# Vision tower kernel: first tile's keys right behind its convolutions, its later steps among the second tile's products

## The chip, the core and the metric

One core of a Trainium2 chip runs the kernel. The metric is device time in microseconds (us), the median of 3 runs. PE is the matrix engine (TensorE), DVE the vector engine, ACT the scalar engine, POOL GpSimd, SP the queue that issues loads and stores.

## What is computed

`x` holds 64 images of 3 x 96 x 96, all weights are float32. A convolution with patches of 14 x 14 gives 6 x 6 = 36 rows of 256 channels for each image. They form 4 windows of 9 rows. Cut to what matters here:

```
red   = mean of the 9 rows of a window
q     = LN(red) @ la_wq ;  k, v = LN(rows) @ la_wkv
agg   = softmax(q . k / 16) over the 9 rows, 8 heads, times v
local = red + agg @ proj_w + proj_b
patch = local @ mod_w + mod_b                       (4 tokens)
cls   = class_emb + attention(class query, LN(local)) @ ga_proj   (1 token)
h     = [cls_tok, patch, cls]                       (6 tokens)
h     = h + causal attention(LN(h)) @ Wp + bp       (16 heads)
h     = h + top-2-of-8 experts(LN(h))
```

## The kernel before

**Rows and tiles.** The 64 images x 4 windows are 256 pairs; two tiles ("wt" 0 and 1) of 128 pairs each. Each tile has 9 convolution tiles of 128 rows, so there are 18, in 6 groups of 3 (`GT`): groups 0 to 2 are the first tile, 3 to 5 the second. Tokens 1 and 2 come from the first tile, 3 and 4 from the second, and 0 and 5 (class) from a third.

**Products in float32r pieces.** Convolutions, keys/values and the experts split each operand into a high and a low piece and sum three products (`PRODUCTS`). ACT writes the high piece (`patches_hi`, `turned`), DVE or POOL subtracts it for the low piece (`patches_lo`, `turned_lo`). `patches_lo(1)` and `(2)` are DVE's, 3 to 5 POOL's (`POOL_FROM`).

**Steps of a group.** PE `conv` (L429), ACT copies the rows out of the bank (`conv_copy`, L804), POOL sums the window (`window_sum`, L1068), DVE takes the moments (`group_moments`, L1197), POOL the reciprocal root (L1054). PE turns the rows (`turn_group`, L453) into banks 2 and 3, ACT and DVE make the two pieces (L845, L1317), PE multiplies by `wkv` (`keys_values`, L506, banks 4 to 7), ACT scales the result out (`keys_values_copy`, L865).

**Steps of a tile.** `window_mean` (DVE) normalises the mean row, `window_query_turn` and `window_query` (PE) give the query, `window_scores`, `score_maximum`, `window_weights` (DVE, L1237 to L1254, with one exponential on ACT) the weights. `value_product` (L355) multiplies values by weights, `value_sum` (L360) adds thirds, `tail_agg` (PE, L549) sums 128 x 128 blocks against the identity. For tile 0 the two sums leave 3 blocks (6 products); for tile 1, 6 blocks (12 products). Then come `tail_proj`, `local_out`, `tail_lo`, `tail_mod`, `pool_normalise`, `tail_pool`, `patch_out`, `in_normalise`, and for the tokens `turn_in`, `tile_qkv` (L628), `attention_products` (L376), `att_scores`, `att_weights`, `token_values` (L367), `turn_context` (L644), `out_proj` (L653), `residual`, `mid_normalise`, `turn_mid`, `router` (L667).

**What sets the order.** Each engine has one program, written out by hand, and runs it in order. Semaphores couple them; for the eight PSUM banks `FILLS` lists who writes a bank in which sequence, and `wait_free` makes the writer wait until all the writers ahead of it in that list have been copied out:

```
def wait_free(eng, b, name):
    n = FILLS[b].index(name)
    if n:
        eng.wait_ge(drained[b], n)
```

In bank 2 the list before runs turn0, turn1, turn2, redT0, turn3, and so on, and `turned_lo(g)` on DVE is what counts a turn as copied out. PE's list before runs: convolutions 0, 1, 2, keys 0, convolutions 3, keys 1, convolutions 4 (with the query of tile 0 between), keys 2, convolutions 5, keys 3, 4 and 5 (class products and the query of tile 1 between), then all that follows the weights of either tile. `keep_clock` (L674) issues products whose result nobody reads. From 130.9 us on runs the loop over 8 experts (L754, L767), with a prologue; the change does not touch it.

**Loads.** SP loads patches three groups ahead of their use, a group's buffer being free once the split of the group three before is done; the first experts' weights follow when all splits are done (issued at 50.3 us).

## Time and profile before

| what | value |
|---|---|
| median of 3 runs | 230.98 us (230.65 to 232.23) |
| the profiled execution's own time | 230.04 us |
| its span (first to last instruction) | 228.3 us |
| granted clock of PE, mean | 0.993 |
| busy PE / DVE / ACT / POOL | 202.4 / 157.0 / 101.3 / 95.7 us |

The span is what the trace covers; the execution's time is 1.74 us longer than it. A timeline row gives the start, the time from there to the end of the last of its merged instructions, the engine, the line, what is written and read, the shape, the count, and in brackets how long the engine stood idle before it and what ended that. Ends of PE rows are modelled, and overlap the next row's start a little: from start to start is the truer measure of a run of products.

### The profile page before, as it was taken

To read this page: it belongs to the slowest core of one execution; us is meant where nothing else is said; L and a number is where in the kernel's file an instruction comes from. 1 tells how busy PE (TensorE), PEld (TensorE's weight loads), DVE (VectorE), ACT (ScalarE), POOL (GpSimd) and SP (SyncE) were. 2 spreads that over 40 slices of the span, in tenths; PEclk is the share of its full clock that TensorE was granted. 3 is DMA by queue.
4 is the path that set the end of the run, shared out by engine and by line. 5 is a ranking of instruction groups with operands and counts; after the bars stand their busy time and mean duration, and the time that the engine had idled before them with its cause. 6 is when DMAs were issued, how large, how long until landed. Compare 5 with 4: busy or idle time off the path is not lost.

```text
span 228.3 us, 3936 instructions
## 1 busy us (share of the span) xinstructions
PE 202.4 (89%) x1332; PEld 186.4 (82%) x1332; DVE 157.0 (69%) x357; ACT 101.3 (44%) x225; POOL 95.7 (42%) x100
## 2 busy tenths in 40 slices
PE   1889979989999965878588889999999999999983
PEld 1888969877988845746376789999999999999983
DVE  2565880668388789477987599577856786867641
ACT  3665581825254633325221177283718371717120
POOL 0046099995236934355554314333333333333200
PEclk9999999999999998899999999999999999999999
DMA  6999920009400000000000004272534253400004
GB/s 219 342 384 372 317 95 3 3 17 364 173 0 1 3 0 0 0 0 0 1 3 0 0 3 157 120 279 38 239 97 179 41 235 82 194 0 0 3 0 69
DMA packets 4890, 23.01 MB, mean 101 GB/s; under 512 B 694, under 2 KB 2444, under 8 KB 3724
## 3 DMA queue, kind: packets, MB, share of 16 engines
q1 hardware_dynamic: 3960, 21.26, 26.8%
q10 hardware_dynamic: 916, 1.58, 2.0%
q8 instruction: 8, 0.13, 0.2%
q14 instruction: 6, 0.05, 0.1%
HBM read 22.44 MB, written 0.39 MB: 100 GB/s over the span
## 4 chain that ended last, share of the span: by engine, by line
PE 60%; DVE 13%; POOL 10%; issue 6%; ACT 4%; DMA 2%; SPq 2%; ACTq 0%; DVEq 0%; POOLq 0%
PE bank L754 25%; PE bank L767 15%; PE bank L506 5%; PE bank L429 4%; POOL split L1083 3%; POOL window L1068 3%; DMA raw<-xb 2%; PE bank L644 2%; DVE kv_rows L1237 2%; POOL rstd L1054 2%; PE bank L549 2%; PE bank L453 2%; DVE window L1211 2%; PE bank L653 1%; SPq L350 1%
## 5 line engine op out<-in xcount | busy, mean ns | idle before, releaser
L754 PE MATMUL bank<-split 128*128 128x322 f32 x384 | 59.2, 314 | 0.6 <-DVE vprod L1565 0.6
L754 PEld LDWEIGHTS bank<-split 128*128 128x128 f32 x384 | 57.6, 188 | 0.9 <-issue 0.9
L1182 POOL TENSOR_TENSOR split<-raw,split 128x256 fp32r<-128x256 f32 x32 | 29.0, 908 | 56.6 <-DVE split L1518 56.6
L767 PE MATMUL bank<-split 128*128 128x256 f32 x288 | 36.1, 283 | 0.6 <-DVE split L1571 0.6
L767 PEld LDWEIGHTS bank<-split 128*128 128x128 f32 x288 | 35.4, 192 | 0.8 <-DVE split L1571 0.8
L429 PE MATMUL bank<-split 128*128 128x256 f32 (+1 forms) x225 | 28.3, 284 | 1.8 <-POOL split L1086 1.2
L429 PEld LDWEIGHTS bank<-split 128*128 128x128 f32 (+1 forms) x225 | 27.5, 191 | 2.5 <-POOL split L1086 1.7
L506 PE MATMUL bank<-split 128*128 128x512 f32 x108 | 26.9, 399 | 0.0
L1021 ACT ACTIVATE vprod<-bank 128x322 f32<-128x322 f32 x32 | 13.9, 436 | 24.7 <-PE bank L754 24.6
L1565 DVE TENSOR_TENSOR vprod<-bank,vprod 128x322 f32<-128x322 f32 x32 | 15.7, 491 | 11.9 <-PE bank L754 8.3
L506 PEld LDWEIGHTS bank<-split 128*128 128x128 f32 x108 | 19.8, 188 | 3.9
L1513 DVE TENSOR_TENSOR split<-raw,split 128x512 fp32r<-128x512 f32 x29 | 20.7, 712 | 2.4 <-ACT split L891 2.3
L1029 ACT CAST split<-vprod 128x322 fp32r<-128x322 f32 x32 | 14.8, 463 | 16.3 <-DVE vprod L1565 16.2
L1054 POOL TENSOR_TENSOR rstd<-veps,mhalf 128x1 f32<-128x1 f32 (+2 forms) x17 | 11.3, 670 | 25.4 <-DVE veps L1204 25.2
L891 ACT CAST split<-raw 128x512 fp32r<-128x512 f32 x32 | 19.5, 614 | 2.6 <-DMA raw<-ffn_w 2.6
L1197 DVE BATCH_NORM_STATS2 stats<-pe_rows 128x6 f32<-128x256 f32 x24 | 9.0, 417 | 14.6 <-ACT pe_rows L804 14.4
L1557 DVE SCALAR_TENSOR_TENSOR pe_rows<-bank,wgt,pe_rows 128x256 f32<-128x256 f32 x24 | 11.2, 479 | 11.1 <-PE bank L767 11.1
L1571 DVE TENSOR_TENSOR split<-vprod,split 128x322 fp32r<-128x322 f32 x32 | 15.9, 497 | 1.4 <-ACT split L1029 1.4
L865 ACT ACTIVATE kv_rows<-bank,rstd 128x512 f32<-128x512 f32 x18 | 12.0, 691 | 8.4 <-PE bank L506 8.4
L1068 POOL TENSOR_TENSOR window<-window,pe_rows 128x256 f32<-128x256 f32 x14 | 11.7, 836 | 9.2 <-ACT pe_rows L804 8.1
L804 ACT COPY pe_rows<-bank 128x256 f32<-128x256 f32 x18 | 6.5, 374 | 19.0 <-PE bank L429 18.1
L444 PE MATMUL bank<-split 128*128 128x256 f32 (+1 forms) x45 | 8.2, 356 | 5.3 <-ACT split L818 5.3
(165 smaller groups left out, 287.4 us busy)
## 6 DMA issues: line engine op xcount, KB each, us to landing
raw<-ffn_w SPq DMA_DIRECT2D x8, 1536.0 KB, 6.5
raw<-xa SPq DMA_DIRECT2D x5, 768.0 KB
tok<-tok_w SPq DMA_DIRECT2D x1, 1536.0 KB, 12.9
tok<-tok_w SPq DMA_DIRECT2D x1, 776.0 KB, 6.7
raw<-xa ACTq DMA_DIRECT2D x1, 576.0 KB, 5.4
raw<-xb SPq DMA_DIRECT2D x6, 96.0 KB
att<-att_w SPq DMA_DIRECT2D x1, 488.0 KB, 14.4
raw<-conv_w SPq DMA_DIRECT2D x1, 384.0 KB, 5.9
```

Of the source, the lines that this page charges most:

```text
L429: mm = pe.matmul(bank[b][:, 0:C], xs[0:n, g % 2, px, a:a + P], cws[0:n, pw, k, :], start=(k == 0 and m == 0), stop=(k == len(KCH) - 1 and ...
L506: mm = pe.matmul(bank[b][:, :], lns[:, g % 2, px, a:a + P], wkvs[:, pw, aw:aw + 2 * C], start=(c == 0 and m == 0), stop=(c == CC - 1 and m ...
L754: mm = pe.matmul(bank[b][:, 0:NCOL], aws[:, q, pw, a:a + P], ms[:, px, c, FIRST:ROWS], start=(c == 0 and m == 0), stop=(c == CC - 1 and m ...
L767: mm = pe.matmul(bank[b][:, 0:C], hids[:, px, s * FQ + q, a:a + P], bws[:, s, pw, q * C:(q + 1) * C], start=(q == 0 and m == 0), stop=(q = ...
L891: act.copy(aws[:, q, HI, :], a_raw[:, slot, q, :]).then_inc(a_hi, 1)
L1029: act.copy(hids[:, HI, s * FQ + q, FIRST:ROWS], hidf[:, q % 2, :]).then_inc(hid_hi, 1)
L1054: pool.tensor_tensor(rstd[0:parts, k, 0:n], veps[0:parts, k, 0:n], mhalf[0:parts, 0:n], ALU.pow).then_inc(rstd_done, 1)
L1068: pool.tensor_tensor(redsum[:, wt, :], pe_rows[:, wt, 0, :] if n == 1 else redsum[:, wt, :], pe_rows[:, wt, n, :], ALU.add).then_inc(sum_s ...
L1182: pool.tensor_tensor(bws[:, s, LO, q * C:(q + 1) * C], b_raw[:, s, q, :], bws[:, s, HI, q * C:(q + 1) * C].bitcast(F32), ALU.subtract).the ...
L1513: dve.tensor_tensor(aws[:, q, LO, :], a_raw[:, slot, q, :], aws[:, q, HI, :].bitcast(F32), ALU.subtract).then_inc(a_split, 1)
L1565: dve.tensor_tensor(hidf[:, q % 2, :], bank[5 + q % 2][:, 0:NCOL], sg[:, q % 2, :], ALU.mult).then_inc(hid_done, 1)
L1571: dve.tensor_tensor(hids[:, LO, s * FQ + q, FIRST:ROWS], hidf[:, q % 2, :], hids[:, HI, s * FQ + q, FIRST:ROWS].bitcast(F32), ALU.subtract ...
```

## The change

PE runs keys 0, 1 and 2 and the query of tile 0 before convolutions 3; ACT and DVE follow. `patches_lo` 3 to 5 go from POOL to DVE, and tile 0's value products and sums too. The steps of tile 0 behind its weights (aggregate, projection, modulation, tokens 0 to 2, their attention, output projection and middle normalisation) are issued between convolutions 4 and the end of keys 5. Tile 1 gets no sums: `tail_agg(1)` takes 9 blocks (18 products) behind three value products on DVE. `token_values` of tokens 0 to 2 go from POOL to DVE. Banks and buffers are dealt out anew (`h0`, `pv0`; `lo` and `poolnorm` hold one tile), and functions that are only moved are not shown.

```diff
--- before.py
+++ after.py
-VSTEPS = 4
+VSTEPS = 5
 REST = KCH[-1][1]
 REST_PARTS = ((0, 64), (64, REST))
-POOL_FROM = 3
 AHEAD_A, AHEAD_B = 3, 2
...
-QKV = {"qkv_cls": (4, (0,)), "qkv0": (7, (1, 2)), "qkv1": (3, (3, 4)), "qkv_pool": (4, (5,))}
+QKV = {"qkv_cls": (2, (0,)), "qkv0": (3, (1, 2)), "qkv1": (3, (3, 4)), "qkv_pool": (4, (5,))}
...
-LNS = ["conv0", "conv1", "conv2", "conv3", "red0", "conv4", "class", "conv5", "red1",
-       "pool0", "pool1", "in0", "in1", "in2", "mid0", "mid1", "mid2"]
+LNS = ["conv0", "conv1", "conv2", "red0", "class", "conv3", "conv4", "pool0", "conv5", "red1", "in0", "mid0",
+       "pool1", "in1", "in2", "mid1", "mid2"]
...
-MOD_BANK = (6, 1)
-LO_BANK = (3, 0)
+AGG_BANK = (6, 2)
+PROJ_BANK = (7, 3)
+LO_BANK = (6, 6)
+MOD_BANK = (1, 7)
...
+    [f"conv{i}" for i in range(TILES) if CONV_BANK[i] == 2] + ["turn0", "turn1", "turn2", "redT0", "turn3", "turn4", "redT1", "turn5",
+                                                            "qkv_cls", "agg1", "poolT1", "wp1", "mid1"],
+    ["turn0", "turn1", "turn2", "q0", "turn3", "turn4", "q1", "turn5", "qkv0", "mid0", "proj1", "qkv1"],
...
-        lo = sb("lo", [P, 2, C])
+        lo = sb("lo", [P, C])
         loT = sb("loT", [P, CC, P])
-        poolnorm = sb("poolnorm", [P, 2, C])
+        poolnorm = sb("poolnorm", [P, C])
+        h0 = sb("h0", [P, C])
+        pv0 = sb("pv0", [P, BLOCKS[0][1] * (BLOCKS[0][1] + 1) // 2, HS * DV])
         poolT = sb("poolT", [P, CC, 2 * P])
...
-            elif g < POOL_FROM:
+            else:
                 eng.wait_ge(x_split, g)
-            else:
-                eng.wait_ge(x_split_pool, g - POOL_FROM + 1)
...
-                    elif wt == 1 and i == 0:
-                        pe.wait_ge(third_done, 2)
-                    elif wt == 1 and i == GT:
-                        pe.wait_ge(vprod_step, VSTEPS + 3)
+                    elif wt == 1 and i % GT == 0:
+                        pe.wait_ge(vprod_step, VSTEPS + 1 + i // GT)
...
             keys_values_group(0)
+            turn_group(2)
+            window_query_turn(0)
+            keys_values_group(1)
+            window_query(0)
+            keys_values_group(2)
             conv_group(3)
-            turn_group(2)
-            keys_values_group(1)
+            class_column()
             conv(GT * 4)
             conv(GT * 4 + 1)
-            window_query_turn(0)
-            conv(GT * 4 + 2)
-            window_query(0)
             turn_group(3)
-            keys_values_group(2)
-            conv_group(5)
-            turn_group(4)
-            class_column()
-            keys_values_group(3)
-            turn_group(5)
             pe.wait_ge(tok_rest_in, 16)
             class_query()
+            conv(GT * 4 + 2)
+            class_keys()
+            conv(GT * 5)
+            tail_agg(0, range(GT))
+            turn_group(4)
+            conv(GT * 5 + 1)
+            tail_proj(0)
+            conv(GT * 5 + 2)
+            tail_lo(0)
+            keys_values(GT * 3)
+            tail_pool(0)
+            tail_mod(0)
+            keys_values(GT * 3 + 1)
+            window_query_turn(1)
+            keys_values(GT * 3 + 2)
+            window_query(1)
+            turn_group(5)
             keys_values(GT * 4)
+            turn_in(0)
             keys_values(GT * 4 + 1)
-            window_query_turn(1)
-            keys_values(GT * 4 + 2)
-            window_query(1)
-            keys_values(GT * 5)
-            class_keys()
-            keys_values(GT * 5 + 1)
-            keys_values(GT * 5 + 2)
...
-            tail_agg(0, range(GT))
-            tail_proj(0)
             pe.wait_ge(att_in, 16)
             pe.wait_ge(tok_cols, 1)
             qkv("qkv_cls")
-            tail_agg(1, (*range(2 * GT, NW), *range(GT)))
-            tail_lo(0)
+            tile_qkv(0, "qkv0")
+            keys_values(GT * 4 + 2)
+            keys_values_group(5)
+            pe.wait_ge(dve_values, BLOCKS[0][1])
+            turn_context(0, 0)
+            out_proj(0, 1, [(0, "ctx0")])
+            turn_mid(0, 3)
+            tail_agg(1, range(NW))
             tail_proj(1)
...
-            pe.wait_ge(pool_values, BLOCKS[0][1])
-            turn_context(0, 5)
-            out_proj(0, 2, [(5, "ctx0")])
-            pe.wait_ge(pool_values, BLOCKS[0][1] + 1)
-            pe.wait_ge(dve_values, 1)
+            pe.wait_ge(pool_values, 1)
+            pe.wait_ge(dve_values, BLOCKS[0][1] + 1)
             turn_context(1, 6)
-            out_proj(1, 0, [(6, "ctx1")])
-            pe.wait_ge(dve_values, 2)
-            pe.wait_ge(pool_values, BLOCKS[0][1] + 2)
+            out_proj(1, 2, [(6, "ctx1")])
+            pe.wait_ge(dve_values, BLOCKS[0][1] + 2)
+            pe.wait_ge(pool_values, 2)
             turn_context(2, 5)
-            out_proj(2, 7, [(5, "ctx2")])
-            turn_mid(0, 3)
-            turn_mid(1, 2)
+            out_proj(2, 7, [(0, "ctx0"), (5, "ctx2")])
             pe.wait_ge(gate_split, 1)
             wait_free(pe, 4, "router")
             router(0, 3)
+            turn_mid(1, 2)
             keep_clock(6, 2)
             router(1, 2)
...
+            keys_values_copy(0)
+            turned(2)
+            two_pieces(2, "redT0", redT, "q_g", "q_b")
             patches_hi(4)
-            keys_values_copy(0)
-            conv_copies(3)
-            turned(2)
+            keys_values_copy(1)
+            query_copy(0)
+            keys_values_copy(2)
+            conv_copy(GT * 3)
+            window_exp(0)
+            conv_copy(GT * 3 + 1)
+            conv_copy(GT * 3 + 2)
             patches_hi(5)
-            keys_values_copy(1)
             conv_copy(GT * 4)
             conv_copy(GT * 4 + 1)
-            two_pieces(2, "redT0", redT, "q_g", "q_b")
+            turned(3)
             conv_copy(GT * 4 + 2)
-            query_copy(0)
-            turned(3)
-            keys_values_copy(2)
-            conv_copies(5)
+            conv_copy(GT * 5)
+            aggregate_copy(0)
             turned(4)
-            keys_values_copy(3)
-            window_exp(0)
+            conv_copy(GT * 5 + 1)
+            conv_copy(GT * 5 + 2)
+            copy_pair(LO_BANK[0], "lo0", loT)
+            keys_values_copy(3, 0)
+            patch_columns(0)
+            keys_values_copy(3, 1)
+            two_pieces(2, "redT1", redT, "q_g", "q_b")
+            keys_values_copy(3, 2)
+            query_copy(1)
             turned(5)
-            two_pieces(2, "redT1", redT, "q_g", "q_b")
-            keys_values_copy(4)
-            query_copy(1)
-            wait_full(act, CONV_BANK[TILES - 1], f"conv{TILES - 1}")
             weights_hi(0, 0, 16)
-            keys_values_copy(5)
...
+            keys_values_copy(4, 0)
+            hT_copy(0)
+            keys_values_copy(4, 1)
+            qkv_copy("qkv_cls")
+            qkv_copy("qkv0")
+            keys_values_copy(4, 2)
+            keys_values_copy(5, 0)
+            attention_exp(0)
+            keys_values_copy(5, 1)
+            keys_values_copy(5, 2)
+            context_copy(0, 0)
             window_exp(1)
+            experts_input_hi(0, 3)
             weights_hi(0, 1, None)
             weights_hi(0, 2, None)
             down_hi(0)
             down_hi(1)
...
-            attention_exp(0)
+            attention_exp(1)
             hT_copy(2)
-            attention_exp(1)
             qkv_copy("qkv_pool")
-            context_copy(0, 5)
+            context_copy(1, 6)
             attention_exp(2)
-            context_copy(1, 6)
             context_copy(2, 5)
-            experts_input_hi(0, 3)
             experts_input_hi(1, 2)
             experts_input_hi(2, 5)
...
-            patches_lo(3)
             window_sum(2)
             reciprocal_root("conv2", GT)
-            patches_lo(4)
+            reciprocal_root("red0", 1)
+            with_proj_bias(0)
+            reciprocal_root("class", 1, 2)
             window_sum(3)
             reciprocal_root("conv3", GT)
-            reciprocal_root("red0", 1)
-            patches_lo(5)
-            with_proj_bias(0)
             window_sum(4)
             reciprocal_root("conv4", GT)
-            reciprocal_root("class", 1, 2)
+            reciprocal_root("pool0", 1)
             window_sum(5)
             reciprocal_root("conv5", GT)
             reciprocal_root("red1", 1)
             with_proj_bias(1)
+            reciprocal_root("in0", 1)
...
+            out_bias(0, MOD_BANK[0], "mod0")
+            reciprocal_root("mid0", 1)
             weights_lo(0)
-            second_tile_third()
-            reciprocal_root("pool0", 1)
...
-            pool.wait_ge(att_step, ATT)
-            for t in (1, 2, 0):
-                values(t)
...
+            def value_products(wt):
+                dve.wait_ge(soft_step, SOFT * (wt + 1))
+                if wt:
+                    wait_full(dve, AGG_BANK[0], "agg0")
+                for k in range(GT):
+                    value_product(dve, wt, k).then_inc(vprod_step, 1)
+
+            def first_tile_sums():
+                for k in (1, 2):
+                    dve.wait_ge(vprod_step, 1 + k if k == 1 else VSTEPS - 1)
+                    value_sum(dve, k).then_inc(vprod_step, 1)
...
+            patches_lo(1)
+            group_moments(0)
+            patches_lo(2)
+            weights_centred()
+            turned_lo(0)
+            group_moments(1)
+            turned_lo(1)
+            group_moments(2)
+            window_mean(0)
+            patches_lo(3)
+            turned_lo(2)
+            dve.wait_ge(con_in, 32)
+            moments("class", [crow[0:2, :]], 2)
+            normalise("class", [crow[0:2, :]], [crow[0:2, :]], 2)
+            patches_lo(4)
+            window_scores(0, 0)
+            window_scores(0, 1)
+            window_scores(0, 2)
+            score_maximum(0)
+            window_weights(0)
+            value_products(0)
+            wait_full(dve, 5, "clsT")
...
+            dve.tensor_tensor(clsT[:, :], clsm[:, :], w_tok("gq_b"), ALU.add).then_inc(cls_step, 1)
+            patches_lo(5)
+            wait_full(dve, 5, "gq")
...
+            dve.tensor_tensor(gqblk[:, :, :], const("headmask").rearrange("p (c h) -> p c h", c=CC),
...
+            first_tile_sums()
+            group_moments(3)
+            wait_full(dve, 5, "u")
...
+            turned_lo(3)
+            group_moments(4)
+            turned_lo(4)
+            local_out(0)
+            group_moments(5)
+            pool_normalise(0)
+            window_mean(1)
             dve.wait_ge(bias_in, 64)
+            patch_out(0)
+            turned_lo(5)
+            in_normalise(0)
+            window_scores(1, 0)
+            dve.tensor_copy(hT[:, 0, :, :, :].rearrange("p c s b -> p c (s b)"), spread(tokT[:, :], 2, P)).then_inc(tok_cols, 1)
+            attention_products(dve, 0, ("qkv_cls", "qkv0")).then_inc(qk_dve, 1)
+            att_scores(0)
+            window_scores(1, 1)
+            att_weights(0)
+            att_wait(0, ATT)
+            for t in (1, 2, 0):
+                values(t)
+            window_scores(1, 2)
+            score_maximum(1)
+            residual(0, 1)
+            residual_moments(0, 1)
             window_weights(1)
+            value_products(1)
+            mid_normalise(0)
+            experts_input_lo(0, 3)
             local_out(1)
             pool_normalise(1)
             patch_out(1)
+            in_normalise(1)
...
-            residual(0, 2)
-            residual_moments(0, 2)
-            residual(1, 0)
-            residual_moments(1, 0)
-            mid_normalise(0)
+            residual(1, 2)
+            residual_moments(1, 2)
             mid_normalise(1)
             residual(2, 7)
```

## Rows read from the trace of the kernel before

**Rows 1.** Stretches (us): busy time (x instructions) of each engine, clock, DMA share, GB/s.

```profile
33.10:80.20 47.10, 44.73 (x279) 39.36 (x279) 29.50 (x64) 21.40 (x43) 33.31 (x33) 1.00 0.18 68
80.20:92.90 12.70, 8.07 (x46) 7.40 (x46) 11.15 (x19) 4.03 (x14) 5.53 (x4) 0.87 0.00 0
92.90:130.90 38.00, 29.82 (x161) 22.90 (x160) 28.37 (x70) 11.04 (x37) 17.57 (x21) 1.00 0.00 1
130.90:228.30 97.40, 92.63 (x672) 91.99 (x672) 67.18 (x161) 45.45 (x97) 27.55 (x30) 1.00 0.30 102
```

**Rows 2.** Timeline of PE: start, us, engine, line, shapes, xcount, idle before and what ended it.

```profile
28.14 0.82 PE L453 MATMUL bank<-con,pe_rows 128*128 128x128 f32 x6
...
28.71 4.34 PE L506 MATMUL bank<-split 128*128 128x512 f32 x18
...
34.30 5.65 PE L429 MATMUL bank<-split 128*128 128x256 f32 x45 [1.25 <-POOL split L1086]
...
49.29 0.44 PE L453 MATMUL bank<-con,window 128*128 128x128 f32 x2 [0.96 <-DVE window L1211]
...
80.24 1.58 PE L549 MATMUL bank<-con,vprod 128*128 128x128 f32 x12
...
88.29 4.54 PE L549 MATMUL bank<-con,vprod 128*128 128x128 f32 x24 [3.87 <-POOL vprod L355]
```

**Rows 3.** Stretches of PE: busy, granted clock, DMA share, GB/s.

```profile
84.40:88.30 3.90, 0.03 (x2) 1.00 0.00 0
88.30:92.30 4.00, 4.00 (x22) 0.61 0.00 0
```

**Rows 4.** Timeline of POOL and DVE, window sum, normalisation, splits.

```profile
34.21 2.49 POOL L1068 TENSOR_TENSOR window<-window,pe_rows 128x256 f32<-128x256 f32 x3
...
37.27 0.86 POOL L1054 TENSOR_TENSOR rstd<-veps,mhalf 128x3 f32<-128x3 f32 x1
...
12.59 1.76 DVE L1294 TENSOR_TENSOR split<-raw,split 128x1536 fp32r<-128x1536 f32 x1 [2.08 <-ACT split L827]
...
14.27 0.55 DVE L1296 TENSOR_TENSOR split<-raw,split 76x384 fp32r<-76x384 f32 x1
...
33.11 1.01 DVE L1317 TENSOR_TENSOR split<-bank,split 128x384 fp32r<-128x384 f32 x2
...
70.32 0.82 DVE L1211 TENSOR_SCALAR window<-window,mv,rstd 128x256 f32<-128x256 f32 x1 [0.67 <-POOL rstd L1054]
```

**Rows 5.** Timeline of PE, products that are moved.

```profile
94.52 1.03 PE L486 MATMUL bank<-tok,loT 128*128 128x256 f32 x4
...
101.00 1.75 PE L628 MATMUL bank<-att,tok 128*128 128x224 f32 x8 [0.51 <-ACT tok L950]
```

**Rows 6.** Timeline of DVE and POOL, scores, values, contention.

```profile
73.36 0.95 DVE L355 TENSOR_TENSOR vprod<-kv_rows,pn 128x768 f32<-128x768 f32 x1
...
75.84 2.53 DVE L1237 TENSOR_TENSOR kv_rows<-kv_rows,window 128x768 f32<-128x768 f32 x1 [1.53 <-ACT window L854]
...
78.41 0.95 DVE L1239 TENSOR_REDUCE sc<-kv_rows 128x24 f32<-128x768 f32 x1
...
108.04 0.74 DVE L1398 TENSOR_REDUCE kv_rows<-vprod 128x72 f32<-128x576 f32 x1
...
116.37 0.83 DVE L367 TENSOR_TENSOR window<-kv_rows 128x640 f32<-128x640 f32 x1
...
80.06 1.99 POOL L1144 TENSOR_TENSOR split<-raw,split 128x512 fp32r<-128x512 f32 x1
```

**Rows 7.** Timeline of DVE, POOL and PE, tail.

```profile
110.81 0.41 DVE L1483 TENSOR_TENSOR pe_rows<-bank,base 128x256 f32<-128x256 f32 x1
...
112.17 0.55 POOL L1054 TENSOR_TENSOR rstd<-veps,mhalf 128x1 f32<-128x1 f32 x1 [1.37 <-DVE veps L1204]
...
122.21 1.58 PE L644 MATMUL bank<-con,window 128*128 128x128 f32 x12 [0.17 <-issue]
...
130.06 0.83 PE L667 MATMUL bank<-gsplit,split 128*128 128x8 f32 x6
```

345 lines of the change are left out of this document (127 added, 218 removed).

## The prediction

> **What bounds the kernel now.** I read the stretches first [rows 1]: from 33.1 to 80.2 us PE is busy 44.7 of 47.1 us, so in the convolutions and keys every product that is added to PE's program lengthens it. From 80.2 to 92.9 it is busy 8.1 of 12.7 us and DVE 11.2: here the second tile's weights are the path. From 92.9 to 130.9 neither is full (29.8 and 28.4 of 38.0): a chain of short steps through all engines. The experts (97.4 us) are products back to back and untouched. Next the timeline of PE for the order and for what ended its waits [rows 2]: 1.25 us for POOL's split and 0.96 us for the normalised mean row in the full stretch, then 3.87 us until the second tile's values were weighted. Last the timelines of DVE, POOL and ACT for what is queued behind what. In short: the experts begin when four things in a row are done: the last keys product (80.2), the second tile's aggregate (92.85), and 38.05 us of tail.
>
> **Part 1, keys 0 to 2 right behind convolutions 2.** Turn 2 is issued at 33.05 and done at 33.6 (28.71 plus 4.34; a turn takes 0.57 from start to start [rows 2]). Next on PE stands the query's turn, redT0. It waits for the mean row: POOL starts the last sums at 29.7, is done 2.9 later, takes two reciprocal roots (0.86 and 0.56), and DVE normalises in 0.82 beside POOL's bias add [rows 4, 7]: 35.1. But redT0 is in bank 2 behind turn2, and turned_lo(2), which frees it, stands on DVE behind patches_lo(3): 1.76 + 0.5, then half of 1.01 [rows 4]. So redT0 goes at 37.7, and PE waits 4.1 us, with keys 1 queued behind, for which all was ready by 31. The old waits of 1.25 and 0.96 go, since convolutions 3 now come after two groups of keys. Net +1.9. Bounds: 0, if the idle stays as it was; +3.6, if the clock falls (rival below).
>
> **Part 2, the splits of groups 3 to 5 from POOL to DVE.** 2.3 us each on DVE in place of POOL's. DVE has room until 80.2 (29.5 busy of 47.1 [rows 1]); the only one that anyone waits for is that of part 1. POOL no longer holds DVE up in this stretch: 0, bounds -0.5 and +0.5.
>
> **Part 3, products moved before the last keys.** tail_agg(0) 12 records for about 1.35 [rows 2]; proj and mod, 4 records each, 0.9 each; qkv_cls and qkv0, 12 records at 1.75 for 8, make 2.4 [rows 5]; the turns lo, pool and in0, eight records or four blocks, 0.75 by redT0's spacing [rows 2]. Together 6.3 us on an engine that is full: all on the path. Bounds 5.6 and 6.5 (modelled ends).
>
> **Part 4, new waits of those products.** I walked the four programs against each other. tail_pool(0) waits for pool_normalise(0), which is queued on DVE behind group_moments(5), and that waits for the copy of the last convolution: 1.1 us idle, with tail_mod(0) and keys behind. turn5 in bank 3 waits for q1's copy 0.3; in0, behind turned_lo(5) on DVE, 0.1; qkv_cls waits for tok_cols behind window_scores(1, 0) 0.3. With less pieces of wait in between, +1.6; bounds 0 and 3. The other steps find their input ready: class products, agg0, proj0, lo0 (DVE reaches each 1 to 3 us ahead). Last keys product: 80.2 + 1.9 + 6.3 + 1.6 = 90.0.
>
> **Part 5, from the last keys to the second aggregate.** Before it took 12.65 us. Now DVE is the queue. It idles until qkv0 is copied out (85.1), then does the attention products (about 0.7) and scores of tokens 0 to 2 (0.74 and three steps of 0.25 [rows 6]), a third of the second tile's scores (0.95 twice [rows 6]), weights (0.9), their values (768 columns where 640 took 0.83 [rows 6], in three parts 1.3), the last third of scores 1.9, the maximum 0.6: it is at 93.9. There residual(0) waits for ctx0 (1.5), its copy (0.5) and out_proj(0) (1.1): 94.6; with its moments 1.3; window_weights(1) only then, 0.8: 96.7. Three value products at 0.95 [rows 6], where POOL has just started weights_lo(0), held back until now by mid0's root. Between rows here: DVE's two-input step took 2.53 beside POOL and 0.95 as a rule, the reduce 0.95 beside POOL also [rows 6]. I take 1.1 for it: 100.7. PE's turn_mid(0) waits for mid_normalise(0), behind all three, and tail_agg(1) behind it starts at 101.35, though the first third was ready at 98.8. It has 36 records in place of 24. PE will have idled nearly 7 us; after 3.9 idle the clock in the trace was 0.61 of full over the next 4 us [rows 3], and 24 records took 4.54 where 12 had taken 1.35 [rows 2]. So 4.05 at full clock and 1.7 for the clock: 5.75, to 107.1. That is 17.1 against 12.65: +4.45. Bounds: +1 (DVE's values overlap better, no contention, no fall) and +7.
>
> The Trainium skill bears on the step of 1.1: its page "SBUF — State Buffer", section "Who interferes with whom", says that a DVE instruction with two SBUF inputs and a GpSimd instruction that reads SBUF exclude each other for the whole instruction, whichever started first. By this rule the other order is as likely a price: had the value product started first, POOL would wait and the step cost nothing (239.2). The trace agrees with the rule as far as it goes (2.53 beside POOL, the reduce untouched).
>
> **Part 6, the tail.** What is gone: patch_out(0) with its moments and in_normalise(0), between pool_normalise(1) and the scores of the class query (about 1.3 by 110.81 to 112.17 [rows 7], and 0.7): -2.0 at gatt. The class row h2 was added at 110.81 [rows 7], held by att_scores(0) and POOL, though its product was ready at 109.2: -1.7. So the class row is normalised 16.7 after the aggregate in place of 20.3. ACT gives some back: attention_exp(1) stands before hT_copy(2), and context_copy(1) before attention_exp(2). turn_context(2) starts at +26.4 in place of +29.35 (122.21 [rows 7]). Then residual and norm of tile 0 are not in the way: the last router products end at +34.05 in place of +38.05 (130.06 + 0.83 [rows 7]). So -4.0, bounds -6 (hT_copy(2) costs nothing) and -2.5.
>
> **Sum**, against the profiled execution, 230.04 us (span 228.3 and 1.74 around it; 0.94 under the median, which I leave): +1.9 + 0 + 6.3 + 1.6 + 4.45 - 4.0 = +10.25, that is 240.3 us.
>
> **Rivals.**
> (a) The clock falls in the first wait too. For it: 3.9 us of idle did it at 84.4 [rows 3], and this one is 4.1 after full work. Against: before the old one PE was also thinly used. Price as there: half clock for about 3.4 us of records, +1.7: 242.0. The Trainium skill's "TensorE: Matmul & The Clock Gate", section "HAM oscillation — how this bites in real kernels", says the clock returns to its lower level after too long a gap and each gap pays anew; with its rule applied to both gaps the time is this one, 242.0.
> (b) The second tile's chain is no longer than it was. DVE finishes the first tile's attention beside the keys, as its 11 us of slack in the full stretch allow, and part 5 costs 0 to 1: 230.04 + 9.8 - 4.0 + 0.5 = 236.3. Against: the attention cannot start before qkv0 at 84.
> (c) Faster: the tail's relief outweighs. Place: the gaps of PE in 80.2 to 130.9, 12.7 us [rows 1]. If the moved products fill what was idle (part 3 costs 1 instead of 6.3, being issued where PE would have waited for DVE anyway), the old 3.87 us wait for POOL's product goes, and the first wait is hidden, the time is 230.04 + 1 - 3.9 - 4.0 = 223. It turns at the point where relief, 8, passes the costs before the aggregate; those I count at 14. Against it: 44.7 busy of 47.1.
> (d) Costs and relief cancel: query wait hidden, part 4 nothing, aggregate at full clock, tail -6: 230.04 + 6.3 + 1 - 6 = 231.3.
>
> **How the numbers follow.** The forecast 0.5, (a) 0.22, (b) 0.18, (c) 0.05, (d) 0.05. A measurement of this kernel tells about 1% from no change. (c) counts as faster; (d) as within 1%; 240.3, (a) and (b) as slower. Range: 236.0, just under (b), to 243.5, above (a) for part 4's upper bound.
>
> **What would show it.** In the changed profile: PE idle for about 4 us near 33.6 to 37.7, ended by DVE's turned_lo (L1317 of before); convolution groups unbroken; about 1 us idle before tail_pool(0); the last keys product at 90 (88 to 92); the second aggregate of 36 records starting near 101, ended by mid_normalise(0), at half clock first; the first expert product near 141. If PE has little idle before 80 and the last keys end near 86, parts 1 and 4 are wrong; if the aggregate starts within 8 us of the last keys, part 5 is; if the experts begin more than 36 or less than 32 us after it, part 6 is.

## The result, and the profile after

| | before | after |
|---|---|---|
| median | 230.81 us (4 runs) | 245.69 us (243.26 to 246.73, 4 runs) |
| ratio | 1 | 1.0643 [1.0585, 1.0702] |
| the profiled execution's own time | 230.04 us | 245.45 us |
| last keys product ends | 80.2 us | 92.4 us |
| second aggregate ends | 92.83 us | 110.14 us |
| first expert product | 130.75 us | 146.15 us |
| granted clock of PE, mean | 0.993 | 0.965 |

Medians are over all executions of a kernel; ratios and their 95% intervals leave out those more than 1.5% above its fastest one. The change makes the kernel slower by 6.4%. The direction was forecast, the size was not: 245.7 us stands above 240.3 and also above the range's end of 243.5.

The stretches of the kernel after, cut at the same four milestones as [rows 1] (columns as there). The experts' stretch is as before; everything is lost ahead of it.

```profile
33.10:92.40 59.30, 53.38 (x316) 46.30 (x314) 41.23 (x89) 27.69 (x60) 14.91 (x21) 0.94 0.14 54
92.40:110.20 17.80, 9.12 (x54) 8.29 (x54) 10.36 (x23) 3.57 (x10) 2.64 (x3) 0.81 0.00 0
110.20:146.20 36.00, 25.70 (x125) 19.27 (x125) 19.98 (x51) 7.28 (x25) 12.88 (x15) 0.95 0.00 0
146.20:243.70 97.50, 92.72 (x673) 92.08 (x673) 67.17 (x161) 45.55 (x97) 27.46 (x30) 1.00 0.29 102
```

The clock columns, 0.94, 0.81 and 0.95, where [rows 1] has 1.00, 0.87 and 1.00, are the first thing to see. The timeline of PE after, in the order in which the prediction walked it:

```profile
37.62 0.66 PE L456 MATMUL bank<-con,window 128*128 128x128 f32 x2 [4.02 <-DVE split L1296]
37.94 6.71 PE L509 MATMUL bank<-split 128*128 128x512 f32 x18
...
45.16 4.48 PE L509 MATMUL bank<-split 128*128 128x512 f32 x18
...
74.52 0.44 PE L456 MATMUL bank<-con,poolnorm 128*128 128x128 f32 x2 [1.40 <-DVE poolnorm L1183]
...
84.43 2.51 PE L592 MATMUL bank<-att,tok 128*128 128x224 f32 x12 [0.27 <-issue]
86.62 5.78 PE L509 MATMUL bank<-split 128*128 128x512 f32 x24
...
103.76 0.69 PE L456 MATMUL bank<-con,pe_rows 128*128 128x128 f32 x2 [6.12 <-DVE pe_rows L1183]
104.24 5.90 PE L550 MATMUL bank<-con,vprod 128*128 128x128 f32 x36
...
129.36 0.99 PE L592 MATMUL bank<-att,tok 128*128 128x224 f32 x4 [1.84 <-ACT tok L910]
131.66 3.90 PE L608 MATMUL bank<-con,window 128*128 128x128 f32 x18 [1.30 <-POOL window L370]
138.17 1.58 PE L608 MATMUL bank<-con,window 128*128 128x128 f32 x12 [1.01 <-DVE window L370]
```

The first wait is there as walked: 4.02 us, ended by DVE's low piece of turn 2. So is the long one before the second aggregate, 6.12 us, ended by the middle normalisation, with 36 records behind it. What the sum did not hold is in the durations: keys 1 took 6.71 us for 18 records where keys 2 behind them took 4.48, and the context turn of the second tile 3.90 for 18.

The stretches of PE after, around the three waits (busy, granted clock, DMA share, GB/s):

```profile
36.00:40.00 4.00, 2.38 (x7) 0.52 0.00 0
40.00:44.00 4.00, 4.00 (x12) 0.63 0.02 4
100.00:104.00 4.00, 0.24 (x1) 0.63 0.00 0
104.00:108.00 4.00, 4.00 (x21) 0.52 0.00 2
126.00:130.00 4.00, 1.39 (x7) 1.00 0.00 0
130.00:134.00 4.00, 2.69 (x13) 0.72 0.00 0
```

Three falls to the lower of the clock's two levels, 1.2 GHz, where [rows 3] shows one. The first two follow 4.02 and 6.12 us of idle. The third follows 4 us in which PE was busy 1.39, with gaps of 0.77, 1.84 and 1.30: no single long one. The 1.95 us that PE waited for the first context at 94.34 brought no fall (granted clock 1.00 from 94 to 98).

The timeline of DVE after, at the first wait and at the long one. In front of the low piece at 36.94 stand the split's 1.75 and 0.54, the queue of part 1. In front of the normalisation at 103.31 stand the three value products.

```profile
34.08 0.80 DVE L1183 TENSOR_SCALAR window<-window,mv,rstd 128x256 f32<-128x256 f32 x1 [0.67 <-POOL rstd L1067]
34.80 1.75 DVE L1273 TENSOR_TENSOR split<-raw,split 128x1536 fp32r<-128x1536 f32 x1
36.47 0.54 DVE L1275 TENSOR_TENSOR split<-raw,split 76x384 fp32r<-76x384 f32 x1
36.94 1.00 DVE L1296 TENSOR_TENSOR split<-bank,split 128x384 fp32r<-128x384 f32 x2
...
99.70 3.68 DVE L357 TENSOR_TENSOR vprod<-kv_rows,pn 128x768 f32<-128x768 f32 x3
103.31 0.40 DVE L1183 TENSOR_SCALAR pe_rows<-pe_rows,mv,rstd 128x256 f32<-128x256 f32 x1
```

### The profile page after: what moved, and what is told of

It reads as the page before. It is cut to its first block, busy times and chain, and to the rows that moved or that the text cites. A ratio compares the mean times of both kernels' runs of the same rounds, so it can differ in the third digit from the quotient of the medians.

```text
span 243.7 us, 3950 instructions
## 1 busy us (share of the span) xinstructions
PE 208.8 (86%) x1344; PEld 191.8 (79%) x1344; DVE 158.9 (65%) x370; ACT 102.0 (42%) x225; POOL 68.9 (28%) x86
## 4 chain that ended last, share of the span: by engine, by line
PE 68%; DVE 12%; issue 6%; POOL 5%; ACT 4%; DMA 2%; ACTq 0%; DVEq 0%; POOLq 0%
PE bank L757 24%; PE bank L770 14%; PE bank L432 8%; PE bank L509 6%; PE bank L550 3%; PE bank L447 3%; PE bank L489 2%; PE bank L456 2%; PE bank L608 2%; DMA raw<-xa 2%; POOL window L1081 2%; PE bank L592 2%; POOL rstd L1067 2%; DVE vprod L357 2%; DVE pe_rows L1183 1%
## 5 line engine op out<-in xcount | busy, mean ns | idle before, releaser
L757 PEld LDWEIGHTS bank<-split 128*128 128x128 f32 x384 | 57.6, 188 | 0.9 <-issue 0.9
L770 PEld LDWEIGHTS bank<-split 128*128 128x128 f32 x288 | 35.3, 192 | 0.8 <-DVE split L1550 0.8
L509 PE MATMUL bank<-split 128*128 128x512 f32 x108 | 29.6, 427 | 0.0
L432 PE MATMUL bank<-split 128*128 128x256 f32 (+1 forms) x225 | 28.9, 286 | 0.0
L509 PEld LDWEIGHTS bank<-split 128*128 128x128 f32 x108 | 21.6, 205 | 4.4
L456 PE MATMUL bank<-con,pe_rows 128*128 128x128 f32 x48 | 8.0, 287 | 7.9 <-DVE pe_rows L1183 7.7
L456 PEld LDWEIGHTS bank<-con,pe_rows 128*128 128x128 f32 x48 | 5.5, 143 | 10.7 <-DVE pe_rows L1183 9.6
L1081 POOL TENSOR_TENSOR window<-window,pe_rows 128x256 f32<-128x256 f32 x14 | 12.6, 897 | 3.2 <-ACT pe_rows L807 2.1
```

What stands on the lines that cost most here:

```text
L432: mm = pe.matmul(bank[b][:, 0:C], xs[0:n, g % 2, px, a:a + P], cws[0:n, pw, k, :], start=(k == 0 and m == 0), stop=(k == len(KCH) - 1 and ...
L456: mm = pe.transpose(bank[b][:, n * P:(n + 1) * P], piece, ident)
L509: mm = pe.matmul(bank[b][:, :], lns[:, g % 2, px, a:a + P], wkvs[:, pw, aw:aw + 2 * C], start=(c == 0 and m == 0), stop=(c == CC - 1 and m ...
L757: mm = pe.matmul(bank[b][:, 0:NCOL], aws[:, q, pw, a:a + P], ms[:, px, c, FIRST:ROWS], start=(c == 0 and m == 0), stop=(c == CC - 1 and m ...
L770: mm = pe.matmul(bank[b][:, 0:C], hids[:, px, s * FQ + q, a:a + P], bws[:, s, pw, q * C:(q + 1) * C], start=(q == 0 and m == 0), stop=(q = ...
L1081: pool.tensor_tensor(redsum[:, wt, :], pe_rows[:, wt, 0, :] if n == 1 else redsum[:, wt, :], pe_rows[:, wt, n, :], ALU.add).then_inc(sum_s ...
```

## The experiments

The theory before they ran: the time is the sum of (1) a wait made by DVE's order, (2) 6.4 us of products moved into a stretch where PE was full, (3) waits from orders on DVE, ACT and the banks around the moved steps, and (4) a fall of the clock for each thin spell. The rivals: the moved products are free and the slow clock or the waits are all; or keys first is itself the loss. The ratio of each run is against the kernel before on the same chip, so ratios are what is to be compared between runs. The first keys (keys 0) start anywhere from 28.11 us (e2) to 30.25 us (e15) in the traces, before the change has any effect; where two traces are compared to within a microsecond, the text counts from there or from the last keys.

| run | what it is | median us | ratio |
|---|---|---|---|
| after | the change | 245.69 | 1.0643 [1.0585, 1.0702] |
| e1_turned_first | after, turned_lo(2) before patches_lo(3) | 240.77 | 1.0429 [1.0335, 1.0524] |
| e2_agg_before_mid | after, tail_agg(1) before turn_mid(0) | 246.84 | 1.0678 [1.0564, 1.0791] |
| e3_filled_wait | after, first wait filled | 242.91 | 1.0539 [1.0424, 1.0654] |
| e4_before_more | before, 24 more products in the full stretch | 235.69 | 1.0187 [1.0058, 1.0317] |
| e5_repaired | after, orders and banks mended | 238.69 | 1.0385 [1.0307, 1.0464] |
| e6_before_filled | before, the wait at 84 us filled | 230.77 | 0.9962 [0.9909, 1.0016] |
| e7_all_filled | after, three waits filled | 241.62 | 1.0478 [1.0402, 1.0554] |
| e8_repaired_filled | e5 with filled waits | 234.85 | 1.0158 [1.0072, 1.0244] |
| e9_before_filled_twice | before, two thin spells filled | 229.07 | 0.9946 [0.9899, 0.9992] |
| e10_keys_first_only | before, keys 0 to 2 first, POOL keeps its splits | 235.33 | 1.0148 [1.0067, 1.0228] |
| e11_keys_first_filled | e10 with e9's fills | 233.82 | 1.0117 [1.0066, 1.0167] |
| e12_residual_later | e8, DVE weights and multiplies before the residual | 234.24 | 1.0123 [1.0034, 1.0211] |
| e13_keys_first_dve | before, keys first, splits on DVE, nothing of the tail moved | 228.71 | 0.9906 [0.986, 0.9951] |
| e14_keys_first_filled | e13 with three fills | 227.57 | 0.9861 [0.9798, 0.9923] |
| e15_third_on_dve | e9 with 5 products in the first fill, the second tile's values all on DVE | 228.56 | 0.9908 [0.9865, 0.9951] |
| e16_all_good | e14 and e15 together | 226.5 | 0.9825 [0.9769, 0.9881] |

### e1_turned_first: is it DVE's order that makes the first wait?

```diff
             window_mean(0)
-            patches_lo(3)
             turned_lo(2)
+            patches_lo(3)
```

> The changed kernel with turned_lo(2) ahead of patches_lo(3) on DVE. Theory (the three clock falls and the queued wait explain the miss): the first wait of PE shrinks from 4.0 us to about 1.8 us, the clock doesn't fall in it, and the keys behind it take 4.1 us in place of 6.4; 2.2 + 2.2 less, 241.0 us against 245.5. Rival (the clock falls whatever the wait, or keys run slow here for another reason, such as late operands): only the 2.2 us of the shorter wait, 243.3. Rival (everything here is absorbed by later waits on DVE): 245.5.

The timeline of PE in e1_turned_first:

```profile
35.53 0.41 PE L456 MATMUL bank<-con,window 128*128 128x128 f32 x2 [1.89 <-DVE split L1296]
35.69 4.38 PE L509 MATMUL bank<-split 128*128 128x512 f32 x18
```

The wait fell from 4.02 to 1.89 us, and keys 1 took 4.38 in place of 6.71: the clock did not fall there. The last keys ended at 87.83 in place of 92.40. So 4.6 us of the loss hung on the order of two steps in DVE's program; half was the wait, half the clock.

### e2_agg_before_mid: is it PE's order that holds the aggregate?

```diff
             out_proj(0, 1, [(0, "ctx0")])
-            turn_mid(0, 3)
             tail_agg(1, range(NW))
+            turn_mid(0, 3)
```

> The changed kernel with PE's turn_mid(0) behind tail_agg(1) in place of ahead of it. Theory (PE's own queue delays the second aggregate): the aggregate starts with the first third of the products, about 100.9 in place of 104.2, and ends when the last third is through, about 106.0 to 107.5 in place of 110.1: 2.6 to 4 us less, 242.2 us against 245.5. Rival (the value products on DVE and the slow clock set the end of the aggregate anyway): under 1 us less, 244.7.

Timeline of PE, and behind it that of ACT, in e2_agg_before_mid:

```profile
100.38 6.62 PE L550 MATMUL bank<-con,vprod 128*128 128x128 f32 x36 [4.15 <-DVE vprod L357]
...
109.95 1.13 PE L489 MATMUL bank<-tok,aggT 128*128 128x256 f32 x4 [2.73 <-ACT aggT L881]
```

```profile
107.25 0.37 ACT L938 CAST split<-bank 128x256 fp32r<-128x256 f32 x1 [11.64 <-PE bank L456]
107.52 1.14 ACT L895 CAST split<-raw 128x512 fp32r<-128x512 f32 x2
...
109.27 0.36 ACT L880 ACTIVATE aggT<-bank,bv 128x128 f32<-128x128 f32 x1
```

A miss. The aggregate began 9.40 us behind the last keys where after's began 11.84 behind them, so 2.4 us earlier (3.9 by the clock of the trace, 100.38 against 104.24, of which 0.5 is an earlier start and 0.9 a cheaper fall in keys 1). Nothing came of it: its copy on ACT is queued behind `experts_input_hi(0, 3)`, which waits for the turn that now comes later, and behind the casts of weights that stand after it. ACT stood idle for 11.64 us with that turn at the head of its queue. One engine's program was put right without the other's.

### e3_filled_wait: what is the fall in the first wait worth?

```diff
             turn_group(2)
+            fill_wait(0, "conv7", 8)
             window_query_turn(0)
```

`fill_wait` waits until the named writer of the bank is copied out and issues 8 products of the identity with 256 columns of constants into it, which nobody reads.

> The changed kernel with 8 products whose result nobody reads put into PE's first long wait, ahead of the query's turn of the first tile; the wait itself stays. Theory (the clock fell because PE stood idle there, and that alone cost 2.2 us): granted clock 1.0 up to 90 us, the 18 records of keys behind it in 4.1 us in place of 6.4, 243.3 us against 245.5. Rival (the slow keys come from somewhere else): the keys stay at 6.4 and the time at 245.5. If the products overrun the wait, up to 0.3 us is given back.

The timeline of PE in e3_filled_wait:

```profile
33.36 3.62 PE L639 MATMUL bank<-con 128*128 128x256 f32 x16
37.55 0.41 PE L456 MATMUL bank<-con,window 128*128 128x128 f32 x2 [0.57 <-DVE split L1302]
37.72 4.35 PE L509 MATMUL bank<-split 128*128 128x512 f32 x18
```

The wait is as long as it was (the query's turn still goes at 37.55), but PE is busy in it. Keys 1 now take 4.35, and the last keys end at 89.81, 2.6 us earlier (2.5 counted from keys 0). That is the price of this fall alone: rival (a), which had 1.7.

### e4_before_more: are added products in the full stretch on the path?

```diff
                 wait_free(pe, b, f"kv{i}")
+                for _ in range(4 if i == GT * 3 else 0):
+                    for c in range(CC):
+                        for m, (px, pw) in enumerate(PRODUCTS):
+                            a, aw = (c * GT + j) * P, 2 * c * C
+                            pe.matmul(bank[b][:, :], lns[:, g % 2, px, a:a + P], wkvs[:, pw, aw:aw + 2 * C],
+                                      start=(c == 0 and m == 0), stop=(c == CC - 1 and m == 2))
```

The added products are the six of one tile, issued four times more; the same products then write the bank again.

> The kernel before, with the six products of the second tile's first key tile issued four more times into the same bank (24 records of 128x512 at about 0.23 us, 5.5 us), in the stretch where PE is full. The result is the same. Theory (products put into this stretch are on the path, one for one): 5.5 us more, 236.3 us against 230.8. Rival (c) of the prediction (the moved products fill time in which PE would have waited): 0 to 2 us more, under 232.8.

24 records of the kind that takes 0.23 us from start to start are 5.5 us. The median was 235.69 (1.0187 [1.0058, 1.0317]). Read at an equal mean clock it is sharper: executions of 234.46 and 234.51 us, both at 0.993, stand against one of the kernel before of 229.33 at 0.992, so +5.1 for 5.5. The trace says the same: from keys 0 to the end of the last keys 56.63 us against 51.45 before, +5.2, at a granted clock of 1.00 in both. Rival (c), in which the moved products cost 1 in place of 6.3, is out: what is added between 33 and 80 us is paid nearly whole.

### e5_repaired: how much is order alone?

```diff
-PROJ_BANK = (7, 3)
+PROJ_BANK = (7, 0)
...
-            turn_mid(0, 3)
             tail_agg(1, range(NW))
             tail_proj(1)
             tail_lo(1)
             tail_mod(1)
+            turn_mid(0, 3)
...
-            experts_input_hi(0, 3)
...
             patch_columns(1)
+            experts_input_hi(0, 3)
...
             qkv_copy("qkv1")
-            attention_exp(1)
             hT_copy(2)
+            attention_exp(1)
             qkv_copy("qkv_pool")
-            context_copy(1, 6)
             attention_exp(2)
+            context_copy(1, 6)
```

and e1's edit, and `experts_input_lo(0, 3)` on DVE behind `patch_out(1)`.

> The changed kernel with its orders mended: turned_lo(2) ahead of patches_lo(3); the first tile's middle turn and its two pieces behind the second tile's modulation on PE, ACT and DVE (the second projection goes to bank 0 so that it doesn't wait for them); hT_copy(2) ahead of attention_exp(1) and attention_exp(2) ahead of context_copy(1) on ACT. Theory (the queued waits cost 2.2, 3 and 3 us beside the clock): last keys at 87.5, second aggregate ended near 102, experts 33 us behind it, 235 us. Rival (the tail and the middle are held by DVE's own work and by the clock, and an order mended in one queue only shows the next one, as with the aggregate moved alone): 239 to 241.

It came to 238.69 and not the 235 expected; by the ratios that is 1.0 us under e1, within the intervals of the two. The rival of the expectation (239 to 241, a mended order only shows the next one) was the nearer. The timeline of PE in e5_repaired tells where the rest went:

```profile
96.99 6.91 PE L550 MATMUL bank<-con,vprod 128*128 128x128 f32 x36 [4.14 <-DVE vprod L357]
...
125.41 3.29 PE L608 MATMUL bank<-con,window 128*128 128x128 f32 x18 [2.68 <-POOL window L370]
```

The aggregate starts 7.25 us earlier than after's, of which 4.65 came with e1's edit; counted from the last keys it is 2.4, as in e2. Then it runs at half clock (6.91 us where 36 records take about 4.2 at full). And with ACT's order mended the context turn waits for POOL's values instead. Mending waits moved the thin spells, it did not remove them.

### e6 and e9: what does filling do for the kernel before?

```diff
             qkv("qkv_cls")
+            fill_wait(7, "kv15", 8)
             tail_agg(1, (*range(2 * GT, NW), *range(GT)))
...
-            keep_clock(6, 4)
+            keep_clock(6, 8)
             turn_in(2)
```

The first edit is e6; e9 has both.

> The kernel before with 8 products whose result nobody reads behind qkv_cls, in the wait of 3.87 us ahead of the second aggregate. Theory (the idle spell made the clock fall and the 24 records behind it took 1.8 us more): the records take 2.7 in place of 4.5, 1.8 us less, ratio 0.992. Rival (the next wait, for the copy of the first projection's rows on DVE, takes it back): ratio 1.0. If the fall moves to a later spell of the tail, also 1.0, and the clock row shows it there.

> The kernel before with unread products in both of its long waits: 8 behind qkv_cls, and keep_clock(6, 4) made keep_clock(6, 8) ahead of the third tile's turn. Theory (with only the first wait filled the fall moved to 113 to 119 us, behind the idle 2.18; filled as well there is none left): granted clock 1.0 in nearly all executions, 228.5 us, ratio about 0.985 to the kernel before, and less spread between executions. Rival (a fall comes in any gap of the tail, as small as 0.5 us): the ratio stays near 0.996.

The stretches of PE in e6_before_filled:

```profile
109.00:113.00 4.00, 1.36 (x8) 1.00 0.00 2
113.00:117.00 4.00, 3.43 (x16) 0.57 0.00 0
```

The aggregate's 24 records took 3.32 us in place of 4.54 [rows 2] (the clock stayed at 1.00), and the time stayed where it was (0.9962 [0.9909, 1.0016]): 20 us later, behind 4 us with PE busy 1.36, stands a fall that the kernel before did not have. The spell itself is not new. In the trace of before it has the same wait of 2.18 us and the same busy time, and there the clock stayed at 1.00:

```profile
110.60:114.60 4.00, 1.36 (x8) 1.00 0.01 2
```

So such a spell can bring a fall and need not; what decides was not found. With that spell filled too (e9) the median was 229.07, 0.9946 [0.9899, 0.9992], and the profiled execution ran at a mean clock of 1.000. That is less than the 0.985 expected: from keys 0 to the first expert product the trace is 1.3 us shorter than before's (100.77 against 102.04), about the one fall. One fill alone is not a measurement of what a fall costs.

### e7 and e8: the change with its waits filled, without and with mended orders

```diff
             turn_group(2)
+            fill_wait(0, "conv7", 8)
             window_query_turn(0)
...
             out_proj(0, 1, [(0, "ctx0")])
+            fill_wait(7, "kv15", 12)
...
             turn_in(2)
+            keep_clock(6, 4)
             tile_qkv(2, "qkv_pool")
+            keep_clock(6, 2)
```

This is e7, on after. e8 stands on e5 and has 3 and 6 products in place of 8 and 12.

> The changed kernel with unread products in all its long waits: 8 in the first, 12 ahead of the first tile's middle turn, 4 and 2 around the third tile's qkv. No order is changed. Theory (the miss of the prediction is the clock: 2.2 us in the first wait, 1.6 in the tail, and the 1.7 it had priced): granted clock 1.0 throughout, aggregate of 36 records in 4.0, turn_context(1) in 2.3, 240.0 us. Rival (only the first fall counts, the others lie beside DVE's work): 243.

> The mended orders and the unread products together (3, 6, and 4 and 2). Theory: two sizes add, the mended orders 10.7 less and no fall of the clock after it about 3 less: 232 us, no faster than the kernel before, since the 6.3 us of moved products on the full stretch stay. Rival: the mended orders alone keep PE busy enough, so no gain over them: 235.

Timeline and stretches of PE in e7_all_filled:

```profile
92.80 2.33 PE L608 MATMUL bank<-con,pv 128*128 128x128 f32 x12 [1.95 <-DVE pv L370]
...
104.32 4.18 PE L550 MATMUL bank<-con,vprod 128*128 128x128 f32 x36
...
130.02 2.27 PE L608 MATMUL bank<-con,window 128*128 128x128 f32 x18 [0.44 <-POOL window L370]
```

```profile
92.00:96.00 4.00, 2.63 (x13) 0.68 0.00 0
96.00:100.00 4.00, 4.00 (x10) 0.50 0.00 0
```

The three falls of after are gone (36 records in 4.18 in place of 5.90, 18 in 2.27 in place of 3.90), and a new one came behind the 1.95 us wait for the first context, a wait that brought none in after. Net 241.62, above the 240.0 expected. e8's trace has a granted clock of 1.00 from 30 us to the experts: 234.85 (1.0158 [1.0072, 1.0244]), above the 232 expected. This is the change with its orders and its clock mended, and it is still slower than the kernel before.

### e10 and e11: is keys first itself the loss?

```diff
             keys_values_group(0)
-            conv_group(3)
             turn_group(2)
+            window_query_turn(0)
             keys_values_group(1)
+            window_query(0)
+            keys_values_group(2)
+            conv_group(3)
```

with turn 3 one convolution earlier, ACT, POOL and DVE in the same order, the splits of groups 3 to 5 left on POOL, and no step of the tail moved. e11 adds e9's fills.

> One part of the change alone, made on the kernel before: keys 0 to 2 and the first tile's query right behind convolutions 2, its scores and weights on DVE as early; turned_lo(2) directly behind the window's mean; POOL keeps its splits and value products; every step behind the first tile's weights stays at its old place behind the last keys. Theory (the loss sits in the moved products, not in the keys' order): first wait of PE 1.9 us in place of 1.25 and 0.96, last keys at 80 as before, POOL's sums of the first tile no longer beside the second tile's scores; 229 to 231 us, ratio 0.99 to 1.0. Rival (keys first itself costs, by a wait of convolutions 3 for POOL's split, which now starts later): 233 to 235.

> The run before it with the unread products of e9 in addition. Theory: the two add, 227 to 228.5 us, ratio 0.98 to 0.985. Rival (the first gap of 1.9 us or a new one at the aggregate lets the clock fall): ratio 0.995.

The first came to 1.0148 [1.0067, 1.0228], the second to 1.0117 [1.0066, 1.0167], where 0.99 to 1.0 and 0.98 to 0.985 were expected: two misses. Timeline of DVE and of POOL in e10_keys_first_only:

```profile
33.82 3.50 DVE L1213 TENSOR_SCALAR window<-window,mv,rstd 128x256 f32<-128x256 f32 x1 [0.67 <-POOL rstd L1056]
```

```profile
33.74 3.42 POOL L1085 TENSOR_TENSOR split<-raw,split 128x1536 fp32r<-128x1536 f32 x1
```

The normalisation of 128 x 256, 0.80 us in after, took 3.50 beside POOL's split, which had begun 0.08 us ahead of it and ended 0.16 us before it; the first wait became 4.60 us. The Trainium skill's page "SBUF — State Buffer", section "Who interferes with whom", says that a tensor_scalar can take both of DVE's port pairs and is then shut out for the whole instruction by GpSimd when that was issued first. This row agrees.

It was no new thing either. The same step of the same tile stood like this in the trace of before, on DVE and on POOL, and ended the 0.96 us wait of [rows 2]; the 0.82 us of [rows 4] is the second tile's, with no split beside it:

```profile
45.68 3.56 DVE L1211 TENSOR_SCALAR window<-window,mv,rstd 128x256 f32<-128x256 f32 x1 [1.29 <-POOL rstd L1054]
```

```profile
45.60 3.48 POOL L1083 TENSOR_TENSOR split<-raw,split 128x1536 fp32r<-128x1536 f32 x1
```

Two more prices stand in e10's trace. Keys 1 behind the longer wait took 6.18 us (granted clock 0.50 from 36 to 40), and convolutions 5 waited 1.64 us for POOL's split and then took 7.14 us for 45 records that take 5.65 in [rows 2] (0.75 from 64 to 68). From e10 to e13, which differ in who makes the splits, the ratio falls by 2.4%, 5.6 us: the move of the splits to DVE, costed at 0 in part 2, is what makes keys first pay.

### e12_residual_later: the last order in the second chain

```diff
-            residual(0, 1)
-            residual_moments(0, 1)
             window_weights(1)
             value_products(1)
+            residual(0, 1)
+            residual_moments(0, 1)
             mid_normalise(0)
```

> The mended and filled kernel (e8) with residual(0) and its moments behind the second tile's weights and value products on DVE. Theory (they stand ahead of the weights in DVE's queue and cost their wait of 1.0, their 1.3 and the POOL contention of 0.7 on the path): the aggregate ends 2 to 3 us sooner, 232.5 us against 234.9. Rival (PE's unread products or the keys' end hold the aggregate): under 0.5 us less.

The second aggregate ended at 100.76 in place of e8's 102.74, so the 2 us were there; but the clock was 0.53 from 104 to 108 in the profiled execution, and the first expert product came only 0.3 us sooner (135.95 against 136.27). The ratio gained 0.35%, within the intervals of the two, and the median of e12 (234.24) is no lower than that of e8 without its one execution of 239.21 at clock 0.964 (234.15). The chain is shorter in the trace; in time nothing is shown.

### e13 and e14: keys first with the splits on DVE

```diff
-POOL_FROM = 3
+POOL_FROM = GROUPS
...
             window_mean(0)
+            turned_lo(2)
+            patches_lo(3)
+            patches_lo(4)
+            window_scores(0, 0)
+            window_scores(0, 1)
+            window_scores(0, 2)
+            score_maximum(0)
+            window_weights(0)
+            patches_lo(5)
+            group_moments(3)
```

on top of e10's order. e14 adds 3 products ahead of the query's turn and e9's fills.

> As e10 (keys and query of the first tile first, all its later steps at their old places), but with the splits of groups 3 to 5 on DVE as in the changed kernel, so that POOL's split no longer stretches the normalised mean row (3.50 us in e10) and convolutions 5 don't wait for POOL (1.64). Theory (keys first is harmless, the changed kernel's loss is in the moved products and in the orders around them): first wait of PE 1.9 us, no other up to the last keys, which end near 79.8; 229 to 232 us, ratio 0.99 to 1.005, 3 to 5 us under e10. Rival (keys first costs whoever makes the splits): 234 to 236.

> The run before it with unread products in its long waits (3 ahead of the first query's turn, 8 behind qkv_cls, 4 more ahead of the third tile's turn). Theory: 228 to 229.5 us, ratio 0.985 to 0.993, as e9, since neither wait nor product differs on the path. Rival: the stretch behind the last keys has changed (POOL's sums of the first tile earlier), and gains another 1 us.

The timeline of PE in e13_keys_first_dve:

```profile
35.39 0.41 PE L453 MATMUL bank<-con,window 128*128 128x128 f32 x2 [1.89 <-DVE split L1316]
...
85.90 4.64 PE L549 MATMUL bank<-con,vprod 128*128 128x128 f32 x24 [3.18 <-POOL vprod L355]
```

0.9906 [0.986, 0.9951] and 0.9861 [0.9798, 0.9923]: the first half of the change, taken alone and with DVE's order right, makes the kernel about 1% faster, inside both ranges expected. From keys 0 to the last keys e13 takes 50.28 us where before took 51.45. The loss sits in the other half, the steps of the first tile placed among the second's products.

### e15 and e16: the version that beats both

```diff
-                    elif wt == 1 and i == 0:
-                        pe.wait_ge(third_done, 2)
-                    elif wt == 1 and i == GT:
-                        pe.wait_ge(vprod_step, VSTEPS + 3)
+                    elif wt == 1 and i % GT == 0:
+                        pe.wait_ge(vprod_step, VSTEPS + 1 + i // GT)
...
-            tail_agg(1, (*range(2 * GT, NW), *range(GT)))
+            tail_agg(1, range(NW))
...
-            second_tile_third()
...
-                for k in range(2):
+                for k in range(GT):
                     value_product(dve, 1, k).then_inc(vprod_step, 1)
-                dve.wait_ge(vprod_step, VSTEPS + 2)
-                value_sum(dve, 1).then_inc(vprod_step, 1)
```

This is the one further piece of the change that looked sound: the second tile's values all on DVE, 18 products in place of 12. e15 has it on e9, e16 on e14, both with 5 products in the fill ahead of the aggregate.

> e9 (kernel before, filled twice; here 5 products in the first wait) with one more part of the change: the second tile's three value products all on DVE, no sum, and 18 products of the aggregate in place of 12. Theory (POOL's product of 2.25 us and the stretched pair of DVE's go, the aggregate streams behind each third): aggregate ends 1 us sooner, 228.0 us against 229.1. Rival (6 more products of PE and DVE's third product cost as much as POOL's did): 229 to 229.5.

> e14 and e15 together: the parts of the change that I take for harmless or good, without the moved products, and with the waits filled. Theory: 227 to 228.5 us, ratio 0.98 to 0.988, faster than both kernels. Rival: no gain over e9, ratio 0.99.

The timeline of PE in e16_all_good:

```profile
84.50 4.18 PE L547 MATMUL bank<-con,vprod 128*128 128x128 f32 x36
```

e15's ratio is 0.4% under e9's, less than the intervals tell apart. Counted from the last keys its aggregate ended after 11.01 us where e9's ended after 11.45: 0.4 us sooner, not the 1 us expected. On top of keys first it is 10.11 us in e16 against 10.43 in e14, and e16 runs in 226.5 us (225.58 to 227.24), 0.9825 [0.9769, 0.9881]: faster than the kernel before by 1.7% and than after by 19 us. Its step from e14 (0.9861) is again within the intervals.

## Why the prediction was right or wrong

By its own steps, in the profiled executions, of +15.4 in place of +10.25:

| step | predicted | measured |
|---|---|---|
| part 1, first wait less the two old ones | +1.9 | 4.02 - 1.25 - 0.96 = +1.8 |
| rival (a), clock in the first wait | 0 in the forecast, 1.7 in the rival | 6.71 - 4.34 = +2.4 |
| part 3, moved products | +6.3 | +6.4, what is left of 12.2 |
| part 4, new waits among them | +1.6 | 1.40 + 0.27 = +1.7 |
| last keys end | 90.0 | 92.4 |
| part 5, last keys to the second aggregate's end | +4.45 | 17.74 - 12.67 = +5.1 |
| part 6, tail | -4.0 | 36.01 - 37.92 = -1.9 |

**Right: parts 1, 4 and 5, and part 3 with some luck.** The wait behind the query's turn was foretold with its cause and its length (4.1 against 4.02), by reading DVE's program against the bank's list of writers; e1 showed that it is this order. The moved products were paid whole (e4: +5.1 for 5.5). Their 6.4 is a remainder, though, and two errors meet in it. From keys 0 to the last keys, e1 and e13, which have the same first wait (1.89 us) and the splits on DVE in both, differ by 8.9 us: PE is busy 7.0 longer (55.40 against 48.39) and idle 1.9 longer, so parts 3 and 4 together had 7.9 for 8.9. And keys first by itself gave 0.9 back that the sum did not hold: e13 takes 1.2 us less than before in this stretch (50.28 against 51.45), of which 0.3 is a shorter wait. That the two nearly cancel was luck. The aggregate was expected at 101.35 and 5.75 us long; it started 11.84 us after the last keys where 11.35 was walked, and took 5.90, of which 1.7 was the clock as priced (4.18 in e7).

**Wrong first: the clock in part 1.** The step was "Against: before the old one PE was also thinly used", on which a fall behind the first wait got a chance of 0.22. A wait of 3.87 us had brought the clock down in the trace of before [rows 2, 3], this one was walked as 4.1, and nothing in the rows said that the second would be spared. It came: clock 0.52 and 0.63 over 8 us, 2.4 us by the rows, 2.6 by e3. The rival should have been the forecast. Its price was short as well: the 18 records of 512 columns behind this wait took 2.4 us more, the aggregate's 24 behind the old one 1.2 more ([rows 2] against e6).

**Wrong second: part 6.** The relief was walked for order and waits, and up to its last third it holds: the class row is normalised 16.9 us after the aggregate, where 16.7 was walked. But `turn_context(2)` starts at +28.0 in place of +26.4, and the last router products end at +36.15 in place of +34.05. Between the two points 1.6 us went to a fall for which the forecast had no term: the context turn of the second tile took 3.90 for 18 records, 2.27 in e7, and e7's whole tail is as much shorter (34.38 against 36.01). The fall came behind small gaps of 0.77, 1.84 and 1.30 us and was gone in e7, where products fill that spell. Only the 1.84 is ACT's order, the other two end on DVE and POOL, and with ACT's order mended (e5) the fall came all the same. Rows of ACT after show that the copy of the class row's turn stood behind the exponential, as the prediction said:

```profile
128.67 0.27 ACT L926 ACTIVATE kv_rows<-kv_rows 128x80 f32<-128x80 f32 x1 [4.31 <-DVE kv_rows L1337]
128.85 0.41 ACT L910 COPY tok<-bank 128x128 f32<-128x128 f32 x2
```

The 0.5 us that remain of part 6 were not traced to a step.

Clock terms together, 2.4 + 1.6, are 4.0 of the 5.2 us missed. The rest is part 5 (0.6) and part 6 (0.5). The range's upper end was built from rival (a) and part 4's bound; it had no case with falls in the first wait and in the tail at once.

**The other rivals.** (b), a second chain no longer than before, fell: +5.1. (c) fell with e4, (d) with part 4 and part 6. The sentence under rival (a) on the Trainium skill's page "TensorE: Matmul & The Clock Gate", section "HAM oscillation — how this bites in real kernels", that each gap pays anew, is borne out by e3 and e7 for the two long gaps; applied to both gaps it gave 242.0, nearer to the result than the forecast. The section behind it on that page, "A second HAM failure mode: psum-queue depth-cycling", tells of a kernel in which frequent short idle spells between groups of products bring the clock down again and again. The stretch 126 to 134 us after, with no gap above 1.84 us, is a case of short spells here; the same spell in before and e6, at 1.00 in one and 0.57 in the other, shows that they do not always do it.

**What the loss is made of, by the runs.** In ratios, from after down: after to e1 2.1% (DVE's order and the fall behind it), e1 to e5 0.4% (orders of ACT, PE and the banks; within the intervals), e5 to e8 2.3% (filled waits), e8 to e14 3.0%. 3.0% of 231 us is 6.9 us. Both e8 and e14 have their waits filled, and both traces show a granted clock of 1.00 from 30 us to the experts, so this pair tells what placing the first tile's steps among the second's products costs when orders and clock are in order. (e8 also keeps the first tile's values on DVE and all three thirds of the second's; e16, which shares the last, stands a little further off, 3.3%.) From the timelines of PE:

| trace | keys 0 to last keys | to the second aggregate's end | to the first expert product |
|---|---|---|---|
| before | 51.45 | 12.67 | 37.92 |
| after | 63.79 | 17.74 | 36.01 |
| e1 | 59.19 | 17.56 | 35.95 |
| e7 | 61.30 | 17.64 | 34.38 |
| e8 | 59.22 | 13.64 | 33.53 |
| e13 | 50.28 | 11.75 | 38.54 |
| e14 | 50.32 | 10.43 | 37.91 |
| e16 | 50.24 | 10.11 | 37.91 |

```profile
83.30 5.80 PE L509 MATMUL bank<-split 128*128 128x512 f32 x24
...
98.48 4.26 PE L550 MATMUL bank<-con,vprod 128*128 128x128 f32 x36 [1.56 <-DVE vprod L357]
```

```profile
76.87 3.02 PE L506 MATMUL bank<-split 128*128 128x512 f32 x12
...
87.11 3.21 PE L549 MATMUL bank<-con,vprod 128*128 128x128 f32 x24
```

The first pair of rows is e8's, the second e14's: their last keys and second aggregates. e8 is 8.9 us longer up to the last keys, 3.2 longer in the second chain and 4.4 shorter in the tail, all three as the prediction had them in sign. The moved steps and their waits in the full stretch cost 8.9 us; what they gave back behind it is 1.2 net.

**Open.** What brings the clock down behind a thin spell in one execution and not in another was not settled; nor was a placement tried in which only some of the moved steps go forward.

## What to carry to other kernels

Work moved out of a chain of waits into a stretch where the engine is full is paid whole, and gives back only what the chain was really waiting for: price both ends before moving it. When a step is moved, walk every engine's program for what is now queued in front of and behind it, the copying engine's as well, because here two steps in the wrong order on DVE cost 4.6 us and one on ACT ate a gain of 2.4. Before taking a duration for a step that moves, look at all rows of that step: the normalised mean row took 0.82 us in one tile and 3.56 in the other. Where a kernel has thin spells of PE, give each a term for the clock and sum them, and judge a filled wait only after looking where the next fall has gone.

## What the runs showed of the hardware that was not expected

- The granted clock fell without any long gap: after 4 us with PE busy 1.39 (gaps up to 1.84 us) after, after 4 us with PE busy 1.36 in e6, and around a wait of 1.64 us in e10 (0.83 and 0.75 from 60 to 68). It does not do so each time: the spell of e6 stands in before with the same 1.36 and a clock of 1.00. A fall cost 1.2 us (24 short records, [rows 2] against e6), 1.6 (18 records, after against e7) or 2.4 to 2.6 us (18 records of 512 columns).
- Filling one thin spell with unread products can bring a fall in a later one that had none: e6 (to 113 us), e7 (to 92), e12 (to 104). Filling both spells of the kernel before gave 0.9946 and a spread of 228.0 to 230.9 us over 12 executions, where the kernel before spread from 229.1 to 235.2 over 22 on the same chip.
- A DVE normalisation of 128 x 256 took 3.50 us in place of 0.80 beside a POOL split begun 0.08 us before it (e10), and 3.56 in the trace of before.
- Between executions of the same kernel the time goes roughly with the mean granted clock: after, 243.26 us at 0.972, 245.45 at 0.965, 246.73 at 0.958, but 245.93 at 0.951. It is not all: at 1.00, e15 ran from 227.52 to 229.91 us, the last with keys 0 starting at 30.25.
